# Layer 0's expert block: GpSimd's scalings and weighted sums in pieces and at other places, gathers held back to tiles 55 and 75

## What is computed

```
h = _layernorm(x, axis=-1) * (1 + cb) + sb
# _L0_ffn_ref: the two best of 8 experts per token, their gates normalised to 1
out_k = gelu(h @ w1[e].T + b1[e]) @ w2[e].T + b2[e]      # for e in the two best
x = x + gb * (out_k * expert_weights).sum(over the two)
```

## Time and profile before

| | |
|---|---|
| median of 3 runs | 1436.42 us (1435.21 to 1439.76) |
| profiled execution | 1436.2 us, of which the span in the trace is 1434.5 us |
| busy in the span | PE 1279.5 us (89%), DVE 1055.6 (74%), ACT 917.6 (64%), POOL 538.4 (38%) |
| mean granted TensorE clock | 0.956 of full speed |

### The profile page before, as it was taken

How to read it: one execution, slowest core, us unless ns; L and a number is a source line. 1 busy time by engine, 2 the same in 40 slices (tenths; PEclk the granted TensorE clock), 3 DMA queues, 4 the chain that set the end, 5 groups by cost and what they waited for, 6 DMA issues and landing times. The chain is left out here.

```text
span 1434.5 us, 28628 instructions
## 1 busy us (share of the span) xinstructions
PE 1279.5 (89%) x9145; PEld 816.4 (57%) x9146; DVE 1055.6 (74%) x2720; ACT 917.6 (64%) x1320; POOL 538.4 (38%) x608
## 2 busy tenths in 40 slices
PE   6999678989886779999999899998999989968898
PEld 3877578979853223343333343433333477768898
DVE  5656366667567588888888789887888847898754
ACT  4565533323355578898888788887888757752232
POOL 5238745466467421222222101222222000788820
PEclk9999679999988999999999999999999989979999
DMA  9960122322326541222222202222220060012210
GB/s 266 215 43 25 35 61 88 102 74 73 86 91 233 150 54 22 42 36 42 42 40 42 39 19 36 42 37 42 42 37 13 5 181 1 26 50 63 65 42 16
DMA packets 112673, 93.96 MB, mean 65 GB/s; under 512 B 20034, under 2 KB 98336, under 8 KB 112544
## 3 DMA queue, kind: packets, MB, share of 16 engines
q1 hardware_dynamic: 101192, 76.18, 24.5%
q0 software_dynamic: 6144, 12.73, 3.0%
q10 hardware_dynamic: 5208, 3.43, 1.0%
HBM read 50.40 MB, written 41.89 MB: 64 GB/s over the span
## 5 line engine op out<-in xcount | busy, mean ns | idle before, releaser
L2446 ACT ACTIVATE probs<-scores_ps 128x1024 f32<-128x1024 f32 x512 | 507.0, 1027 | 88.3 <-PE scores_ps L2473 81.0
L2473 PE MATMUL scores_ps<-q_pack,k_pack 64*128 64x512 f32 x1024 | 245.9, 493 | 37.7 <-ACT probs L2446 23.1
L2490 PE MATMUL pv_ps<-probs,v_pad 128*32 128x512 f32 x2048 | 276.0, 612 | 0.1
L2473 PEld LDWEIGHTS scores_ps<-q_pack,k_pack 64*128 64x128 f32 x1024 | 96.4, 185 | 310.9 <-issue 152.4
L2366 POOL TENSOR_TENSOR squares<-sparse_scores 128x512 f32<-128x512 f32 x32 | 41.0, 1280 | 476.3 <-DVE sparse_scores L2611 476.2
L1406 ACT ACTIVATE hidden_experts<-pre_experts 128x512 f32<-128x512 f32 x94 | 59.3, 631 | 129.6 <-DVE pre_experts L1340 71.0
L2683 DVE TENSOR_SCALAR_CACHE_REDUCE junk<-sparse_scores,at 128x1024 f32<-128x1024 f32 x96 | 122.7, 1279 | 3.4
L1428 PE MATMUL up_ps_experts<-x_t_experts,up_weights_now_experts 128*128 128x128 f32 x752 | 107.1, 288 | 17.9 <-ACT hidden_experts L1406 8.1
L1428 PEld LDWEIGHTS up_ps_experts<-x_t_experts,up_weights_now_experts 128*128 128x128 f32 x752 | 94.8, 198 | 23.5 <-DVE up_weights_now_experts L1335 14.0
L1435 PE MATMUL down_ps_experts<-weights_t,hidden_experts 128*128 x736 | 98.5, 278 | 0.0
L3277 POOL DMA_INDIRECT expert_rows_dram<-expert_input_tail,send_to_tail x64 | 65.0, 1015 | 86.4 <-DVE expert_input_tail L3421 68.9
(11 more groups left out here) (416 smaller groups left out, 2543.7 us busy)
## 6 DMA issues: line engine op xcount, KB each, us to landing
q_pack<-q_pieces_dram SPq DMA_DIRECT2D x120, 64.0 KB
k_pack<-k_pieces_dram SPq DMA_DIRECT2D x120, 64.0 KB
expert_rows_dram<-zeros SPq DMA_DIRECT2D x1, 6400.0 KB, 22.1
x_rows_experts<-expert_rows_dram SPq DMA_DIRECT2D x25, 256.0 KB
expert_rows_dram<-y_rows_experts SPq DMA_DIRECT2D x46, 128.0 KB
q_pieces_dram<-q_pieces_prep SPq DMA_DIRECT2D x8, 512.0 KB, 3.6
k_pieces_dram<-k_pieces_prep SPq DMA_DIRECT2D x8, 512.0 KB, 4.0
expert_rows_dram<-zeros SPq DMA_DIRECT2D x1, 2640.0 KB, 36.4
```

The source lines that it names most:

```text
L2446: act.activation(probs[:, kt % 2, 2 * pair : 2 * pair + 2, c * 512 : c * 512 + 512], scores_ps[n % 2][:].rearrange("p (h t) -> p h t", h=2 ...
L2473: ins = pe.matmul(scores_ps[n % 2][:, head * 512 : head * 512 + 512], k_pack[group % 2][rows, pair, kt * P : kt * P + P].bitcast(F32R), q_ ...
L2490: ins = pe.matmul(pv_ps[32 * j : 32 * j + 32, c, :], v_pad[:, group % 2, kt, j, :], probs[:, kt % 2, j, c * 512 : c * 512 + 512], start=(k ...
```

## The change

1. Batch 2's scaling goes from the start of the expert block to the front block. `scale_and_shift_part` does it in eight pieces (four quarters of the batch, first multiplied, then added to), and `FRONT_ORDER` has them as `hq.2.0` to `hq.2.7`, behind batch 1's last scatter.
2. Batch 3's scaling goes from behind batch 2's scatters to between them: one of the eight pieces after each of the first eight scatters and its wait for a tile.
3. `weighted_sum` works on half a batch at a time (10 instructions for 5).
4. `tile_at` is at least 55 before batch 1's gathers and at least 75 before batch 2's (`GATHERS_FROM`).
5. VectorE's statistics of batch 0 begin at tile 56 for tile 52 (`STATS_AT`).

```diff
+QUARTERS = 4
+    def scale_and_shift_part(self, pool, step, b, i):
+        at = b * NT + i % QUARTERS * (NT // QUARTERS)
+        h = self.h[:, at : at + NT // QUARTERS, :]
+        if i == QUARTERS:
+            step.settle()
+        op, by = ((ALU.mult, CB), (ALU.add, SB))[i // QUARTERS]
+        step(pool.tensor_tensor(h, h, bc(self.mod0[:, b, MOD0_PARTS.index(by), :], NT // QUARTERS), op))
...
-sd.1.12 sd.1.13 sd.1.14 sd.1.15 wk.10 ce2.3.1 ...
+sd.1.12 sd.1.13 sd.1.14 sd.1.15 hq.2.0 hq.2.1 hq.2.2 hq.2.3 hq.2.4 hq.2.5 hq.2.6 hq.2.7 wk.10 ce2.3.1 ...
...
-    STATS_AT = (13, 20)
+    STATS_AT = (14, 20)
+    GATHERS_FROM = (0, 55, 75)
...
                 for b in range(B):
                     if b >= SENT_EARLY:
-                        moe.scale_and_shift(pool, step, b)
                         step.settle()
-                        moe.send_rows(g, pool, b, apart=next_tile)
+                        for i in range(SEND_PARTS):
+                            moe.send_rows(g, pool, b, i, SEND_PARTS, apart=next_tile)
+                            if b + 1 < B and i < 2 * QUARTERS:
+                                moe.scale_and_shift_part(pool, step, b + 1, i)
...
-                    tile_at[0] = max(tile_at[0], (b + 1) * moe.tiles)
+                    tile_at[0] = max(tile_at[0], (b + 1) * moe.tiles, GATHERS_FROM[b])
...
-                        for part in weighted_sum(g, picked, b, NT):
+                        for part in weighted_sum(g, picked, b, NT // 2):
```

More of the change, by code:

```diff
@@ L195 @@
 lg.2.1 wk.18 wt.8 lgk.2.1 h2t.3.0 wt.7 wt.4 wk.8 lg.3.0 wk.7 wt.14 lgk.3.0 wk.12 wk.14 wk.4 rs2.3.1 sd.1.6 sd.1.7 sd.1.8 sd.1.9 sd.1.10 sd.1.11
-sd.1.12 sd.1.13 sd.1.14 sd.1.15 wk.10 ce2.3.1 no2.3.1 tu2.3.1 h2t.3.1 lg.3.1 lgk.3.1 be.1 po.1 exps gates ix.1 te.1
+sd.1.12 sd.1.13 sd.1.14 sd.1.15 hq.2.0 hq.2.1 hq.2.2 hq.2.3 hq.2.4 hq.2.5 hq.2.6 hq.2.7 wk.10 ce2.3.1 no2.3.1 tu2.3.1 h2t.3.1 lg.3.1 lgk.3.1 be.1 po.1 exps gates ix.1 te.1
 """
@@ L615, in scale_and_shift, with scale_and_shift_part @@
                     moe.scale_and_shift(pool, step, b)
+                def scale_and_shift_part(b, i):
+                    if i == 0:
+                        for h in range(2):
+                            wait_made(pool, "tu2", b, h)
+                    moe.scale_and_shift_part(pool, step, b, i)
                 def send(b, q):
@@ L635, in _ @@
                         h2=scale_and_shift,
+                        hq=scale_and_shift_part,
                         sd=send,
```

## The result

The changed kernel takes **1428.41 us** (median of 7 runs, 1424.38 to 1430.47); the kernel before, run beside it on the same chip, 1436.42 (7 runs). The ratio is 0.9947, 95% interval 0.9931 to 0.9963: 0.5% faster, 8.0 us won where 13.6 were forecast. The profiled execution of the changed kernel took 1430.47 us, its span is 1428.7.

The account below looks back on a forecast made before the run. TensorE bounds the expert block, except for 25 us lost to slow stretches while GpSimd computes and standstills behind DMA bursts. Terms +1.5 + 0.2 + 0.5 - 6.4 - 1.6 - 6.6 - 1.2 + 0 = -13.6 us: 1422.8 us, range 1415 to 1431.

Parts of the forecast that it names:

- What bounds the block: Expert block: TensorE sets the pace, 1.926 us a tile; 25 us lost to slow stretches and standstills are all to win.
- The front block's chain: Front block: batch 2's scaling beside VectorE's chain delays five of its operations by 0.3 us each, +1.5 us.
- Batch 3's pieces: Scaling pieces between batch 2's scatters: GpSimd just keeps up, pieces may delay VectorE operations, +0.5 us.
- Scaling and first burst: Tiles 16 to 24: the 1.0 us up to tile 18 and the standstill behind it both go, -6.4 us.
- The sums by halves: Beside batch 0's and batch 1's sums: shorter operations save half of the loss, -1.6 and -1.2 us.
- Second burst: Batch 1's gathers from tile 55 on: paced by tiles, no burst, the standstill goes, -6.6 us.
- Third burst: Batch 2's gathers from tile 75 on: burst only moves ten tiles later, keeping its 5.4 us, 0 won.
- The end of the block: GpSimd's last work ends about 1 us after tile 91, covered by SyncE's last store with over 1 us to spare.
- The first (all three bursts go): Rival, expert block: batch 1's sum ends by tile 75, so the third burst goes too; 1417.9 us, chance 0.25.
- The second (standstills not made by bursts): Rival, expert block: every batch of DMAs costs a standstill wherever it starts; 1434.8 us, chance 0.10.
- The third and fourth: Rivals: one of the first two standstills stays, about 1429 us (0.08); short operations shut VectorE out, 1454 us (0.05).

Follow-up runs that it names:

- The full-width kernel: Changed kernel with its weighted sums again over a whole batch (5 operations for 10), on the second chip: 1423.93 us, ratio 1.004 to the kernel before.
- the first experiment: Changed kernel with four explicit GpSimd drains after the landing of batches' scatters and gathers: 1425.22 us, ratio 0.9927 to the kernel before.
- the kernel with eleven gathers: Changed kernel with batch 2's gathers held back to tile 71, not 75: 1427.06 us, ratio 0.9933 to the kernel before.

## Why the prediction was right and wrong, step by step

**What bounds the block** was right: tiles run at 1.926 us wherever GpSimd neither computes long nor sends a burst, and the loss of some 25 us was all that could be won. The block won 14.2.

**The front block's chain**, +1.5 forecast: +1.5 measured. By kind of operation the picture was coarser than the forecast's. A single-input operation (L851, 0.64 us, 0.18 before) was delayed, and so was a small one with two inputs in SBUF (L856, 0.74 and 0.18), but a larger one with two inputs was not (L817, 0.29 as before, while the scalings ran), and a still larger one a little (L827, 0.57 and 0.42). The Trainium skill (SBUF — State Buffer, section "Who interferes with whom") has operations with two inputs in SBUF contend with a GpSimd instruction that reads SBUF, and single-input ones untouched outside certain modes; by that rule the forecast's term was 3.9. The trace agrees for L856 and in part for L827, not for L817, and the chain's total decides for 1.5.

**The front block's drain** was not in the forecast at all: +1.3 us, as the experiment with the scaling back in the block shows.

**Batch 3's pieces**, +0.5: tiles 0 to 16 took 32.42 us, before 228.56 - 196.96 = 31.60, so +0.8. The sum is near, the reason is another, and that is luck. The pieces stand beside tiles 0 to 8, and these take 16.20 us, before 16.18: the pieces themselves cost nothing that can be seen. The 0.8 comes in tiles 8 to 16, behind three scatters that follow each other at 214.61, 215.90 and 217.39, since GpSimd had fallen about one scatter behind by tile 8, where the forecast had it keep up. That these scatters cause the loss is argued from where it lies and from the second chip: with the same pieces and scatters and full-width sums, tiles 0 to 16 take 31.59 us there.

**Scaling and first burst**, -6.4: 5.4 us won, with 1.0 us still lost in tiles 16 to 24, behind three scatters at 231.03, 232.30 and 233.77. The full-width kernel has the same three on the second chip, and takes 15.43 us for these tiles, so this 1.0 is most likely a small standstill too.

**The sums by halves**, -1.6 and -1.2: undersized. Between tiles 48 and 54 the loss fell from 3.1 to 0.2 us and between 64 and 70 from 2.6 to nothing, though batch 1's sum now stands beside tiles 71 to 78; and the full-width experiment puts the halves alone at 1.5 to 2.3 and 3.3 us. I had taken half of the loss; all but a little of it goes.

**Second burst**, -6.6: right (6.6 lost before, 0.4 now, between tiles 54 and 56). **Third burst**, 0 won: right, at the place forecast (near tile 77, seven gathers), though a little dearer: tiles 76 to 91 lose 7.1 us.

**The end of the block** is the step that failed. The prediction said of GpSimd's last work: "Covered with over 1 us to spare; without that cover, its excess would count in full." Its last operation did end where forecast, at 384.86 + 1.78 = 386.64. But behind it stands the drain of 6.58 us, and the spare microsecond became an excess of 5.4. The trace of before held the row among the queue's own instructions; I had read only the engines' work and the last store, since the drain was hidden there behind ten microseconds of tiles. Against the forecast's -13.6 the profiled executions differ by -5.7: the end gives +5.4 of the gap, the front's drain +1.3, the block +1.1 (its terms sum to -15.3, and it won 14.2). What is left over, within 0.2 us, comes from parts that the change does not touch: the chain starts 0.8 us earlier, the first rows arrive 0.4 earlier than reckoned, and the rest of the program is 1.2 longer. These small ones, and the block's 1.1, are no larger than what separates two profiles of one kernel; the end's 5.4 is the same in both pairs. The medians differ by -8.0, and the range, 1415 to 1431, holds the time.

**The rivals.** The first (all three bursts go) needed the sum to end by tile 75; it ended at 77. The second (standstills not made by bursts) is refuted on the chip with the same DMAs at another spacing, yet it holds one grain: a burst alone is not enough, the chip must be of the kind. The rule behind it, in the same section of the Trainium skill, that TensorE waits for no other engine and DMA contends with no compute engine, agrees with the second chip. On the first and the third TensorE does stand still beside DMAs, though no run shows that SBUF is the place. The third and fourth did not happen: from 199 to 232 us, beside and behind batch 3's pieces, no weight copy takes more than 0.60 us.

**What stays open** is how a burst stops the others. In the changed kernel TensorE and ScalarE show it like this, around the step to tile 81:

```profile
357.23 0.60 PE L1442 MATMUL xt_ps_experts<-ident,x_rows_experts 128*128 128x128 f32 x4
...
364.45 2.07 PE L1448 MATMUL up_ps_experts<-x_t_experts,up_weights_now_experts 128*128 128x128 f32 x8 [5.74 <-ACT x_t_experts L1419]
```

```profile
363.73 0.60 ACT L1419 ACTIVATE x_t_experts<-xt_ps_experts 128x512 f32<-128x512 f32 x1 [5.05 <-remote]
```

The transposes are on record as done by 357.83, and ScalarE, which waits for just them, starts at 363.73, released by something that the profile calls remote. Matmul ends are modelled, so either TensorE stopped inside its work or its signal was late; no run here tells these apart. The matmuls behind the pause are also slow (2.07 us for eight, 1.06 at full pace), at a mean granted clock of 0.90 over the stretch and of 0.57 from 364 to 368 us. Why a burst is followed by this on one chip and not on another is open as well.

## What to carry to other kernels

Before you move an engine's work towards the end of a block, read the queue's own rows there, the drain above all, and not only the engine's operations: a hidden instruction of the old trace is a term of the new sum. Cut long GpSimd operations that run beside VectorE's, and pace its DMAs with the consumer, since a GpSimd that comes late catches up in a burst, and where a burst is moved its cost moves with it on a chip that shows standstills. Time a change on more than one chip before a gain of one per cent is believed or given up.

## What the runs showed of the hardware

- GpSimd's drain at a block's end goes with the number of indirect DMAs that it has sent since its last drain, though all have landed: 0.05 to 0.06 us after none (two later blocks of the changed kernel), 1.35 after 16, 2.68 after 32, 5.28 after 64 (in the tail), 6.58 after 80. From 16 to 80 that is (6.58 - 1.35) / 64 = 0.082 us each. Two drains read longer, 2.43 us after 16 gathers in the first experiment and 4.10 after 16 in the block behind the experts; both were begun while GpSimd still computed, and from the end of its last operation they are 1.34 and 1.4 us. SyncE's drain beside it took 13 ns. The Trainium skill (VectorE: DVE Perf Modes, section "The DRAIN you can't avoid") tells of drains before and after a kernel's own work, on all engines, of about 12 ns. Those here stand at the end of a block, which that section does not treat: SyncE's is of that length, GpSimd's is not.
- The same program with bursts of eight and four DMAs took 1451.97 us on one chip and 1420.33 on another, one run each, at the same granted clock of 1.00 in the stretch shown; behind it, from 240 to 244 us, the clock on the first is 0.65. The kernel before took 1435.7 to 1436.6 on three chips and 1416.5 on the fourth.
- On one chip, eleven and three gathers back to back gave a longest tile step of 11.2 and 3.4 us; seven, in the changed kernel, gave 5.7. Part of this is the clock: behind a pause of 5.7 us in TensorE's work, the granted clock was 0.57 over 4 us in the changed kernel, and 0.50 over 12 us in the kernel with eleven gathers.
